# Experts' scores with the gate's weights standing still, in a fused two-layer kernel

## The reference, cut to what matters

```python
def _L1_ffn_ref(x, gate_w, ln_gamma, ln_beta, fc1s, b1s, fc2s, b2s):
    ...
    scores = xf @ gate_w.T
    scores = (jnp.tanh(scores) + 1.0) * 0.5
    vals, idx = jax.lax.top_k(scores.T, k)
    ...
x = x + _L1_ffn_ref(_layernorm(x, axis=-1), L1_ffn_gate_w, ...)
```

## Time and profile before

| | us |
|---|---|
| median of 3 runs (lowest, highest) | 1471.42 (1470.21, 1471.47) |
| span of the profiled execution | 1470.0 |
| PE, DVE, ACT, POOL busy in the span | 1280.7, 925.6, 465.3, 325.8 |

### The profile page before, as it was taken

How to read it: one execution, slowest core, us unless ns; L and a number is a source line. 1 busy time by engine, 2 the same in 40 slices (tenths; PEclk the granted TensorE clock), 3 DMA queues, 4 the chain that set the end, 5 groups by cost and what they waited for, 6 DMA issues and landing times. The chain is left out here.

```text
span 1470.0 us, 17444 instructions
## 1 busy us (share of the span) xinstructions
PE 1280.7 (87%) x5222; PEld 768.4 (52%) x5222; DVE 925.6 (63%) x3439; ACT 465.3 (32%) x837; POOL 325.8 (22%) x598
## 2 busy tenths in 40 slices
PE   4677968999999899899989989999887719999996
PEld 3444644465466455546545554645444516666764
DVE  6647789767767776865677786686987382211110
ACT  2544432042324315213431521343132433233221
POOL 3121221023112203201220320222102303332331
PEclk9677989999999999989999999999998858999999
DMA  9002000200300400030030003003000025453321
GB/s 293 9 15 59 18 1 22 51 18 15 88 18 1 102 18 1 25 79 18 1 102 17 1 16 87 16 2 87 7 1 1 30 93 173 109 145 87 90 37 18
DMA packets 44904, 72.51 MB, mean 49 GB/s; under 512 B 8101, under 2 KB 26760, under 8 KB 44682
## 3 DMA queue, kind: packets, MB, share of 16 engines
q1 hardware_dynamic: 38666, 62.87, 14.6%
q0 software_dynamic: 6144, 8.52, 3.3%
HBM read 58.27 MB, written 13.07 MB: 49 GB/s over the span
## 5 line engine op out<-in xcount | busy, mean ns | idle before, releaser
L773 POOL TENSOR_SCALAR ve<-mv 128x2 f32<-128x2 f32 x74 | 16.6, 225 | 552.9 <-DVE mv L1041 552.8
L1604 PE MATMUL ps<-x,keys 128*128 128x512 f32 x256 | 127.0, 620 | 0.5 <-DVE hT L1133 0.4
L1761 PE MATMUL ps<-hT,values 128*128 128x512 f32 x256 | 118.2, 592 | 0.0
L2189 PE MATMUL experts_ps<-experts_yT,experts_fc 128*128 128x512 f32 x256 | 111.9, 595 | 1.2 <-ACT experts_yT L2114 1.2
L2201 PE MATMUL experts_ps<-experts_fc,experts_hT 128*128 128x256 f32 x512 | 112.0, 379 | 0.8 <-ACT experts_hT L2126 0.8
L1604 PE MATMUL ps<-zT_second,w 128*128 128x512 f32 x224 | 102.3, 598 | 7.8 <-ACT big L1552 7.2
L2201 PEld LDWEIGHTS experts_ps<-experts_fc,experts_hT 128*128 128x128 f32 x512 | 96.6, 190 | 14.6 <-ACT experts_hT L2126 1.6
L1604 PE MATMUL ps<-w,big 128*128 128x256 f32 x448 | 98.9, 380 | 0.8 <-ACT big L1552 0.8
L2098 DVE SCALAR_TENSOR_TENSOR experts_o<-experts_ps,experts_wh,experts_b2w 128x256 f32<-128x256 f32 x32 | 15.5, 484 | 128.7 <-PE experts_ps L2201 128.7
L2126 ACT ACTIVATE experts_hT<-experts_ps,experts_b 128x512 f32<-128x512 f32 x64 | 44.0, 687 | 155.4 <-PE experts_ps L2189 155.4
L1604 PEld LDWEIGHTS ps<-w,big 128*128 128x128 f32 x448 | 84.3, 190 | 13.8 <-ACT big L1552 1.6
(11 more groups left out here) (435 smaller groups left out, 2489.7 us busy)
## 6 DMA issues: line engine op xcount, KB each, us to landing
gT<-expert_gates SPq DMA_DIRECT2D x16, 1024.0 KB, 9.6
experts_fc<-in_fc1T SPq DMA_DIRECT2D x8, 1024.0 KB, 5.2
experts_fc<-in_fc2T SPq DMA_DIRECT2D x8, 1024.0 KB, 8.7
xT<-in_xT SPq DMA_DIRECT2D x8, 512.0 KB, 3.5
x<-in_x SPq DMA_DIRECT2D x8, 512.0 KB, 3.5
expert_table<-tb SPq DMA_DIRECT2D x7, 528.0 KB, 7.6
out_x<-x SPq DMA_DIRECT2D x7, 512.0 KB, 6.9
w<-in_W SPq DMA_DIRECT2D x2, 1024.0 KB, 9.4
```

The costliest lines, as they stand in the source:

```text
L773: nc.gpsimd.tensor_scalar(o, i, c, None, ALU.add).then_inc(*tick(*event))
L1604: last = nc.tensor.matmul(o, l, r_, start=start, stop=stop)
L1761: last = nc.tensor.matmul(bank("O2", k), S["values"][:, c, k * P:(k + 1) * P], hT[:, c % RING, :], start=(c == 0), stop=(c == HC - 1))
L2189: last = nc.tensor.matmul(g_bank(m), fc1[e % 3][:, k, m * P:(m + 1) * P], yT[e % 2][:, k, :], start=(k == 0), stop=(k == DC - 1))
```

## The change

For batches 0 to 6 the two operands change places. The gate's weights (128 by 8) are stationary and the token tile (128 by 128) moves. The scores then come out with the experts on the partitions, and tile t is given the partitions 32t to 32t+8 of bank 6, so that the four tiles lie on four column tiles of the array (new use SG). The loops are swapped, too: k outside, t inside. ACT copies the 104 by 128 block to a piece of zT, and one PE transpose with a 104 by 104 identity turns it back (use SC, now in bank 7; ST is now in bank 6). That transpose and the four tanh are a new step, `turn_scores`, which is put into the lists behind `route_experts`: in batches 0 to 3 behind `mlp` 0 and ahead of `film` 0, in batch 4 behind `film` 0, in batch 5 between `mlp` 2 and `film` 1, in batch 6 behind the transposes of batch 7's `scores` 1. The diff shows the entries of batches 4 and 6. Batch 7 keeps the old form.

```diff
-    (LAST, 5, "film", 0), (MID, 5, "picked", 1), (LAST, 4, "shift_scores"), (LAST, 4, "table"), (LAST, 5, "film_in", 0), (MID, 6, "mlp", 1),
+    (LAST, 5, "film", 0), (LAST, 4, "turn_scores"), (MID, 5, "picked", 1), (LAST, 4, "shift_scores"), (LAST, 4, "table"), (LAST, 5, "film_in", 0), (MID, 6, "mlp", 1),
...
-    (LAST, 7, "scores", 0), (LAST, 6, "route_experts"), (LAST, 7, "scores", 1), (LAST, 6, "table"), (LAST, 7, "route_experts"),
+    (LAST, 7, "scores", 0), (LAST, 6, "route_experts"), (LAST, 7, "scores", 1), (LAST, 6, "turn_scores"), (LAST, 6, "table"), (LAST, 7, "route_experts"),
...
-    last += [(("O3", h), 6 + h) for h in HALVES] + [(("xt3", h), 6 + h) for h in HALVES] + [(("SC",), 6), (("ST",), 7)]
+    last += [(("O3", h), 6 + h) for h in HALVES] + [(("xt3", h), 6 + h) for h in HALVES] + [(("SG",), 6), (("SC",), 7), (("ST",), 6)]
...
+        scored = slice(0, 3 * 32 + E1)
+        gathered_scores = zT1[scored, 0, 0:P]
...
             def route_experts(b):
+                if room(b) is usual:
+                    evacuate(b, gathered_scores, bank("SG")[scored, 0:P], "SG")
+                else:
+                    turn_scores(b)
+
+            def turn_scores(b):
                 w = room(b)
                 a.wait_ge(*w.uses.at(b, "filled", "SC"))
-                sc = place(w, "SC")[:, 0:NT * E1].rearrange("p (t e) -> p t e", t=NT)
+                apart_ = 32 if w is usual else E1
+                sc = place(w, "SC")[:, 0:NT * apart_].rearrange("p (t e) -> p t e", t=NT)[:, :, 0:E1]
...
+                if w is usual:
+                    product(b, "SG", parts=[(bank("SG")[32 * t:32 * t + E1, 0:P], S["gate_w"][:, k, :], w.zT[:, k, t * P:(t + 1) * P],
+                                             k == 0, k == DC - 1) for k in range(DC) for t in range(NT)])
+                    return
...
+            def turn_scores(b):
+                pe.wait_ge(*at(b, "emptied", "SG"))
+                transposes(b, "SC", parts=[(bank("SC")[:, 0:scored.stop], gathered_scores, ident[scored, scored])])
```

More of the change, by code:

```diff
@@ L171 @@
     (MID, 1, "weigh"), (LAST, 0, "route_experts"), (MID, 1, "picked", 1), (LAST, 1, "film_in", 0), (ATTEND, 2, "spread"),
-    (LAST, 1, "film_in", 1), (MID, 2, "relu", 0), (MID, 2, "mlp", 0), (LAST, 1, "film", 0), (MID, 2, "relu", 1), (LAST, 0, "table"),
+    (LAST, 1, "film_in", 1), (MID, 2, "relu", 0), (MID, 2, "mlp", 0), (LAST, 0, "turn_scores"), (LAST, 1, "film", 0), (MID, 2, "relu", 1), (LAST, 0, "table"),
     (LAST, 1, "fold"), (MID, 2, "relu", 2), (LAST, 1, "turn"), (MID, 2, "relu", 3), (MID, 2, "mlp", 1), (LAST, 1, "product", 0),
@@ L196 @@
     (LAST, 3, "shift_scores"), (MID, 4, "picked", 1), (LAST, 3, "route_experts"), (ATTEND, 5, "spread"), (LAST, 4, "film_in", 0),
-    (LAST, 4, "film_in", 1), (MID, 5, "mlp", 0), (LAST, 4, "film", 0), (MID, 5, "mlp", 1), (MID, 5, "relu", 0), (LAST, 3, "table"),
+    (LAST, 4, "film_in", 1), (MID, 5, "mlp", 0), (LAST, 3, "turn_scores"), (LAST, 4, "film", 0), (MID, 5, "mlp", 1), (MID, 5, "relu", 0), (LAST, 3, "table"),
     (MID, 5, "relu", 1), (MID, 5, "relu", 2), (LAST, 4, "fold"), (LAST, 4, "turn"), (LAST, 4, "film", 1), (MID, 5, "relu", 3),
@@ L239 @@
     (MID, 7, "relu", 1), (LAST, 6, "film", 0), (LAST, 5, "scores", 0), (LAST, 5, "scores", 1), (MID, 6, "picked", 1), (MID, 7, "mlp", 1),
-    (LAST, 5, "route_experts"), (LAST, 5, "shift_scores"), (MID, 7, "mlp", 2), (MID, 7, "relu", 2), (LAST, 6, "film", 1),
+    (LAST, 5, "route_experts"), (LAST, 5, "shift_scores"), (MID, 7, "mlp", 2), (LAST, 5, "turn_scores"), (MID, 7, "relu", 2), (LAST, 6, "film", 1),
     (LAST, 6, "film_in", 1), (LAST, 6, "fold"), (MID, 7, "relu", 3), (LAST, 5, "table"), (LAST, 6, "turn"), (MID, 7, "relu", 4),
@@ L1589, in _ @@
                       "weigh": weigh, "film": film, "transform": transform, "back": back, "hold": hold, "norm_ffn": norm_ffn,
-                      "ffn": ffn, "gelu": gelu, "scores": scores, "route_experts": route_experts, "table": table})
+                      "ffn": ffn, "gelu": gelu, "scores": scores, "route_experts": route_experts, "turn_scores": turn_scores, "table": table})
             a.wait_ge(sc_in, 80)
@@ L1608, in transposes @@
                 pe.wait_ge(*uses.open_(b, *use))
-                for o, i in parts:
-                    last = nc.tensor.transpose(o, i, ident[:])
+                for o, i, *eye in parts:
+                    last = nc.tensor.transpose(o, i, *(eye or [ident[:]]))
                 last.then_inc(*uses.tick("filled", *use))
@@ L1875, in _ @@
                        "back": back, "ffn": ffn, "gelu": gelu, "ffn_out": ffn_out, "scores": scores,
-                       "route_experts": route_experts, "table": table})
+                       "route_experts": route_experts, "turn_scores": turn_scores, "table": table})
             pe.wait_ge(sums_cast, 2)
```

## The result

The changed kernel took 1480.1 us (median of 14 executions, 1471.1 to 1481.2) against 1471.2 for the kernel before (14 executions, 1468.6 to 1472.6): a ratio of 1.0054, 95% interval 1.0043 to 1.0065. The forecast was 1474.0 with a range up to 1478.5, so it is slower than the whole range. Twelve executions lie between 1477.6 and 1481.2, with a mean granted clock of 0.920 to 0.924; the other two took 1471.1 and 1471.3, at 0.930 and 0.929. That the times of one program go with PE's clock is a first sign of where the time went.

What follows compares the result with a forecast made beforehand. PE was taken as busiest (87%), but around the scores it waits for DVE's means or nearly. 0 + 0 + 2.0 + 0.75 = 2.75 us on 1470.0 gave 1472.75, median 1.4 above: 1474.2, called 1474.0; range 1467.5 to 1478.5.

Steps and rivals of the forecast that it cites:

- 0.9 us was taken: Scores' block on PE: expected length per batch in the new form, against 1.78 us before.
- the lower bound of 0.8: Scores' block: 16 records at 0.051 us each, the price of 32-column loads with 16 moving columns.
- Rival C: Scores' block: the tiles do not overlap, 2.7 us instead of 1.8; +3.5, total 1477.5 us; chance 0.07.
- so I count 0: PE time freed by the shorter scores, about 6 us in seven batches: worth 0, since waits for DVE take its place.
- The copy and transpose: 0: ACT's new copy (at most 0.36 us) and the PE transpose (about 0.45) fall into idle time or waits: 0.
- The bound of +0.3 for batch 0: Batches 0 and 1: transpose and tanh ahead of `film` 0 change each by -0.2 to +0.3 us; 0 taken.
- +2.0 was said: Batch 4: moved tanh delay ACT's table and copies, so `film` 1 is late; +2.0 us, ends +0.5 and +2.6.
- wait of 2 to 3 us for amT: Batch 4, expected sign: PE waits 2 to 3 us for ACT's amT; without such a wait the prediction is wrong.
- the low end of +0.5: Batch 4 at full clock: `film` 0's matmuls take 1.98 instead of 3.78 us, and all comes 0.5 us later.
- +0.75 said: Batch 6: the tanh move from idle time into ACT's gapless stretch; +0.75 us, ends +0.7 and +1.0.
- 2.75 us was forecast: Sum of the terms: 0 + 0 + 2.0 (batch 4) + 0.75 (batch 6) on a span of 1470.0 us.
- Rival A: Batches 0, 1 and 3: PE idles longer ahead of `film`, the clock falls; +3 to 6, about 1478 us; chance 0.22.

Runs made afterwards that it cites:

- e3: The changed kernel with the 16 records of the scores issued three times over (48 records): 1471.0 us, ratio 1.0006.
- e5: The changed kernel with a second set of the scores' 16 records, all on one column tile, ahead of its own: 1475.9 us, ratio 1.0039.
- e6: The changed kernel with matmuls of no use in PE's wait for the means ahead of `film` 0, batches 1 to 4: 1470.3 us, ratio 1.0002.
- e1: The scores' matmuls as in the kernel before, but the four tanh in the changed kernel's places: 1471.4 us, ratio 1.0010.
- e7: The kernel before with the same matmuls of no use ahead of `film` 0 as e6: 1472.9 us, ratio 1.0022.
- e2: The changed kernel with transpose and tanh put earlier, batch 4's ahead of `film` 0, batch 6's ahead of batch 7's transposes: 1477.1 us, ratio 1.0043.
- e4: The changed kernel with the scores' 16 records in another order, one column tile's four records behind one another: 1480.5 us, ratio 1.0068.
- e8: The changed kernel run once more with nothing altered: 1478.9 us, ratio 1.0054.
- e11: The changed kernel shifted by 1.7 us, by four matmuls of no use in batch 0's `ffn_out`: 1482.2 us, ratio 1.0093.
- e14: The changed kernel shifted by 0.86 us, by two matmuls of no use in batch 0's `ffn_out`: 1475.4 us.
- e9: The changed kernel with both e6's matmuls of no use in the wait and e2's early tanh: 1470.9 us, ratio 1.0008.
- e10: e9 with the 16 records of the scores issued three times over: 1465.8 us, ratio 0.9981.
- e16: e10 with five matmuls of no use instead of four in batch 3's wait, batch 4's scores issued five times: 1465.0 us, ratio 0.9966.
- e13: e10 shifted by 1.7 us, by four matmuls of no use in batch 0's `ffn_out`: 1468.6 us, ratio 0.9990.
- e15: The kernel before shifted by 0.86 us, by two matmuls of no use in batch 0's `ffn_out`: 1473.7 us.
- e12: The kernel before shifted by 1.7 us, by four matmuls of no use in batch 0's `ffn_out`: 1479.1 us, ratio 1.0055.

## Why the prediction was wrong

**The scores' matmuls: the price was near, the worth was not.** 0.9 us was taken and 0.62 measured, below the lower bound of 0.8: four column tiles at once were not in the rows that gave the bound. Rival C did not hold: 16 records took 0.62 us, not 2.7. The rule that the Trainium skill gives on weight loads (TensorE: Matmul & The Clock Gate, Part 3, What overlaps and what doesn't), that they overlap with running matmuls only where the row group differs, did not hold either: all four tiles share the rows of the array, and the 16 loads lie beside the matmuls. The 2.7 us were a bound of the prediction, from loads of 128 columns.

The step that failed is "so I count 0", the worth of the PE time that comes free. PE did wait for DVE in the time gained, as argued (in batch 1 0.85 us at the gates and 1.24 us at `film`), and `film` 0 still started 0.15 us behind the means there. But the freed time was not worth 0; it cost. The low stretches came to lie on work of PE that nothing hides: 1.6 us on xf,fd of batch 0, 3.2 at 1073 us, 1.5 near 1230. That this hangs on the work ahead of the waits is shown by medians: e3, with nothing but more records of the scores, is 0.48% faster (7 us), e5 0.15%, e6 with matmuls of no use in the wait 0.52%; and e1, the old matmuls with the tanh moved, has no such loss. How idle time leads to low clock is not shown. In batch 0 of the changed kernel PE waited 0.99 us for the gates and the clock was low behind it; in batch 1 it waited 0.85 and then 1.24 us and the clock stayed full; e6 kept the low stretches of batch 0; and in e7 the same fill did nothing for the kernel before.

**The copy and transpose: 0, held in part.** The copy is 0.25 us, in time when ACT waits for PE. The Trainium skill (TensorEngine Tiling (Array Packing), Performance Considerations, PSUM Bottleneck) says that the copy out of PSUM may become the bottleneck; in this trace it did not. In batch 0, at half clock, `film` 0 starts 0.42 us behind the means, and the tanh stand ahead of the copy of the means and hold DVE for 1.39 us; `film` 1 then waits 0.80 us for DVE, and xf,fd starts 1.1 us later behind the scores' start than before. The bound of +0.3 for batch 0 was too low for that.

**Batch 4: the chain as read, its worth in part luck.** The tanh were expected 7.92 us behind the scores' start (884.75 - 876.83) and came 7.92 us behind it. DVE was expected to stand 3 us and stood 2.98. The table came 4.7 us behind the copy of the means. +2.0 was said, +2.3 measured. But PE had no wait of 2 to 3 us for amT (0.46), which the prediction had named as a sign that it is wrong: PE's own matmuls ran at half clock until the same moment, so ACT was not the only one that was late. With the tanh early (e2) only 0.4 us of the 2.3 came back. e3, with full clock there, has 14.69 us against 14.41, near the low end of +0.5.

**Batch 6: right in place, high in size.** +0.75 said, +0.52 by the table's start; all four tanh lie in ACT's gapless stretch. From the scores of batch 6 to the end the kernels with late tanh and the scores once took 312.3 to 313.0 us in six traces (after, e1, e4, e8, e11, e14) and 310.5 in the seventh (e6), those with early ones 309.5 to 310.2. The rest, about 1.5 us, is one more low stretch, near 1230 in the changed kernel.

**The sum.** 2.75 us was forecast from the order. Averaged over three positions, the moved tanh cost 2.8, but this agreement is partly luck: the three differences are 1.6, 2.4 and 4.6 us, e1 against the kernel before gives 1.5, and with the wait filled (e6, e9) there is none. What was left out is at this position larger: low clock. Rival A had the mechanism (the shorter block leaves PE idle, the clock falls) and was given 0.22 and 3 to 6 us; the measured excess over the forecast was 6.1. Its detail was off: `film` of batches 0 and 1 was not slowed as in batch 2, but xf,fd of batch 0, batch 3's film and work 700 us later were. It was argued against by the 128 streamed columns of the new form: with 16 such records batch 0 had low clock on xf,fd, with 48 it had none in e3, e10 and e16, and in e13 it had some. The other argument was that batch 3 had idled without a fall of the clock. That was a wrong reading of the kernel before: PE waited only 0.50 us there, and its xf,fd in batch 3 did run at low clock, 5.35 us instead of 3.86:

```profile
763.98 5.35 PE L1604 MATMUL ps<-xf,fd 128*128 128x256 f32 x16 [0.91 <-DVE xf L1215]
```

**The base.** The sum was set on the profile of before as if its low clock were a property of its order. e15 and e12 show that it is in part a property of its position: with 0.86 and 1.7 us ahead of it, the same kernel takes 0.24% and 0.55% more, 3.5 and 8 us, more than the shift. So a part of the loss, 0.54% at this position against 0.32% on average, may be a lead that the kernel before had at its own place. On average the change cost 4.7 us, give or take 1.7, where 2.8 was forecast, and there the miss, 1.9 us, is about as large as the uncertainty. The trace of before alone does not show that.

Not settled: which idle time the clock answers to (the wait for the gates or that for the means; e9 against e6 and e10 leaves it open), what in a shift moves the low stretches, and why executions of one kernel differ behind batch 4 (after against e8).

## What to carry to other kernels

Where PE waits in every stage, look at the granted clock by stage before pricing a saving: here time that became idle on PE came back as half clock on the work behind it. Before a difference of less than 1% is put down to a change, shift the kernel before by a microsecond; if it moves by as much, the comparison is between positions. And a few matmuls of no use in a wait on PE are a cheap thing to try: here they took the changed kernel from 0.54% above the kernel before to level with it (e6), and together with more records and earlier tanh to 0.19% (e10) and 0.34% (e16) below. In the kernel before they cost 0.22% (e7).

## What the runs showed of the hardware that had not been expected

fp32 matmuls with 8 stationary and 128 moving columns cost 0.109 us a record on one column tile and 0.0275 on four, in either order of the tiles (0.62 and 0.65 us for 16). PE's busy time alone did not tell its clock: 1.92 us of 8-column matmuls in batch 0 of the kernel before were followed by clock 0.50, 1.50 us of 128-column ones in e3 by full clock. A shift of all layers from batch 0's `ffn_out` on changed the time by more than the shift, at the same work in the same order: by the ratios the changed kernel by -3.8 us at 0.86 us, the one before by +3.5 at 0.86 and +8 at 1.7. One and the same program up to batch 4 ran it with a low stretch on batch 0's xf,fd in one execution (e6) and at full clock in another (e9).
